# A graph network on one core: rounds of eight tables instead of twelve in the count stage

## The reference

```python
edge_index = jnp.stack([src, dst])                   # row = src, col = dst
h = jnp.maximum(_layernorm(x), 0.0)
deg = jnp.bincount(row, length=n)
norm = deg_inv_sqrt[row] * deg_inv_sqrt[col]
agg = segment_sum(norm[:, None] * h[col], row, n)    # what the count stage makes
x = x + relu(agg @ W.T + b)
h = jnp.maximum(_layernorm(x), 0.0)
edge = concatenate([h[src], h[dst], edge_attr_16])
h2 = relu(relu(edge @ W1 + b1) @ W2 + b2) @ W3 + b3
return x + h + segment_sum(h2, dst, n) / maximum(cnt, 1)[:, None]   # cnt: edges per dst
```

## Time and profile before

| | us |
|---|---|
| median of three runs | 6202.02 (6193.15 to 6207.08) |
| the profiled execution, whole | 6196.43 |
| its span, first to last instruction | 6194.6 |
| busy in the span: PE, DVE, POOL, ACT | 5140.4, 3557.7, 4065.8, 1693.7 |
| first build matmul of the count stage starts | 507.3 |
| first unit matmul starts (round 13) | 655.5 |
| units alone begin | 1949.5 |
| the stage after the count stage begins (POOL) | 2053.35 |

### The profile page before, as it was taken

One profiled execution on the slowest core, in us unless ns is written; L12 is line 12 of the kernel. 1 busy time (PEld: TensorE's weight loads), 2 busy tenths in 40 slices (PEclk: granted clock), 3 DMA queues, 4 the chain that ended last, 5 costly groups with the idle time before them and its releaser, 6 DMA issues. The chain is left out here.

```text
span 6194.6 us, 148888 instructions
## 1 busy us (share of the span) xinstructions
PE 5140.4 (83%) x40298; PEld 4289.9 (69%) x40299; DVE 3557.7 (57%) x11420; ACT 1693.7 (27%) x3084; POOL 4065.8 (66%) x3903
## 2 busy tenths in 40 slices
PE   3885999999999768887778888878888778888887
PEld 3883899999998656666666666666666666666666
DVE  8998999999996544434433443434443434443444
ACT  3226666666663221111111111111111111111110
POOL 2005666666664467777777777777777777777776
PEclk9998999999999878888888888888888888888888
DMA  9206999999999743333333333333333333333332
GB/s 164 32 0 150 272 290 288 288 291 292 289 291 266 163 112 84 84 84 85 84 84 83 85 84 84 83 85 83 85 83 85 83 85 83 85 83 84 84 85 66
DMA packets 653785, 816.41 MB, mean 132 GB/s; under 512 B 426282, under 2 KB 471052, under 8 KB 653114
## 3 DMA queue, kind: packets, MB, share of 16 engines
q1 hardware_dynamic: 478251, 592.65, 33.0%
q0 software_dynamic: 175360, 221.63, 17.2%
HBM read 563.36 MB, written 250.47 MB: 131 GB/s over the span
## 5 line engine op out<-in xcount | busy, mean ns | idle before, releaser
L1677 POOL DMA_INDIRECT p_got<-p_tab,idx_d x3128 | 2958.5, 946 | 972.2 <-issue 895.0
L1663 ACT ACTIVATE h<-z,b_col 128x512 f32<-128x512 f32 x782 | 537.4, 687 | 3390.8 <-PE z L1803 3332.8
L1667 DVE TENSOR_TENSOR h<-z,nb 128x512 f32<-128x512 f32 x782 | 540.7, 691 | 1595.2 <-PE z L1643 1582.6
L1637 PEld LDWEIGHTS z<-ident_f,p_got 128*128 128x128 f32 x3128 | 422.5, 163 | 1352.0 <-DMA p_got<-p_tab,idx_d 1185.4
L1637 PE MATMUL z<-ident_f,p_got 128*128 128x128 f32 x3128 | 601.2, 324 | 753.8 <-DMA p_got<-p_tab,idx_d 753.6
L1022 PE MATMUL a_ps<-tile_r,pair_l 128*128 128x288 fp8e5 x5280 | 1041.6, 287 | 75.8 <-DVE tile_r L1109 47.5
L859 POOL DMA_INDIRECT sum_tab<-val_s,idx_s x496 | 787.0, 1587 | 469.7 <-ACT val_s L976 331.5
L1643 PEld LDWEIGHTS z<-w_sb,h 128*128 128x128 f32 x6256 | 1044.7, 237 | 58.0
L1043 PE MATMUL out_ps<-gw,a_got 121*128 121x144 bf16 x11340 | 1078.1, 225 | 4.8 <-DMA a_got<-a_tab 4.7
L1643 PE MATMUL z<-w_sb,h 128*128 128x128 f32 x6256 | 1033.8, 320 | 0.0
L985 ACT CAST stage<-a_ps 128x576 uint16<-128x576 f32 x1320 | 837.4, 639 | 406.0 <-PE a_ps L1022 399.1
(11 more groups left out here) (200 smaller groups left out, 3693.2 us busy)
## 6 DMA issues: line engine op xcount, KB each, us to landing
a_tab<-stage SPq DMA_DIRECT2D x330, 576.0 KB
a_got<-a_tab SPq DMA_DIRECT2D x330, 576.0 KB
rel<-rel_row SPq DMA_DIRECT2D x391, 192.0 KB
p_got<-p_tab,idx_d POOLq DMA_INDIRECT x3128
ef<-in_edge_t SPq DMA_DIRECT2D x391, 64.0 KB
q_win<-q_tab SPq DMA_DIRECT2D x782, 24.0 KB
src_bc<-src_row SPq DMA_DIRECT2D x124, 128.0 KB
a_tab<-big SPq DMA_DIRECT2D x22, 472.5 KB
```

The lines of the kernel that those rows point to most:

```text
L1637: pe.matmul(out_tile, p_rows[:, j, :], ident_f[:, :], start=False, stop=False, is_transpose=True, skip_group_check=True)
L1677: pool.indirect_dma_start(p_rows[:, j, :], None, p_tab, bass.IndirectOffsetOnAxis(idx[:, j:j + 1], 0)).then_inc(landed, 16)
```

## The change

ROUND goes from 12 to 8. What follows from it:

- A round has 8 tables: two blocks of four, so two stage buffers in turn and two blocks in `a_got`, where there were three; 16 turns instead of 24; 8 gathers per super-block. `pair_l` gets four buffers instead of three.
- Tables go from 110 rounds of 12 (1320) to 154 rounds of 8 (1232), super-blocks from 10 to 14. LAG stays 13 rounds.
- The tiles left over rise: SG goes from 124 side groups to 168 (672 tiles). There is exactly one side group in each round, the double ones are gone. Groups 154 to 166 are worked on in the 13 rounds that have no tables, and group 167 behind the last round.
- The places inside a round move: pick at 4, mix at turn 10, sum at turn 14, and so on.

```diff
-ROUND = 12
+ROUND = 8
-    MORE_EACH = 7
-    two_sides = range(LAG, ROUNDS, MORE_EACH)
-    assert len(two_sides) == SG - ROUNDS and two_sides[-1] < ROUNDS
+    assert ROUNDS + LAG < SG <= ROUNDS + LAG + 1
-            pair_l = [sb(f"pair_l{k}", [P, P, 2 * WIN_TILES], BF16, life) for k in range(3)]
+            pair_l = [sb(f"pair_l{k}", [P, P, 2 * WIN_TILES], BF16, life) for k in range(ROUND // 2)]
-                PICK_AT = 6
-                MOVE_AT = 8
-                NUMBER_AT = 9
-                MIX_AT = 14
-                SUM_AT = 18
-                MIX_KEPT_AT = 6
-                VAL_KEPT_AT = 8
-                EARLY, LATE = -3, 2
+                PICK_AT = 4
+                MOVE_AT = 6
+                NUMBER_AT = 7
+                MIX_AT = 10
+                SUM_AT = 14
+                MIX_KEPT_AT = 4
+                VAL_KEPT_AT = 6
...
-                    for r in range(ROUNDS):
+                    for r in range(SG):
...
-                        for e, _ in placed(r, sides(r)):
-                            scatter(e)
+                        scatter(r)
...
-                    sweep(sp, DW, LAG - 1, sides, body)
+                    sweep(sp, DW, LAG - 1, body)
+                    for e in range(ROUNDS + LAG, SG):
+                        load_src(e)
+                        load_g(e)
...
+                            if turn_of == MIX_AT:
+                                mix_rows(r)
+                            if turn_of == SUM_AT:
+                                sum_rows(r)
...
-                    sweep(pe, DW, LAG, sides, body)
+                    sweep(pe, DW, LAG, body)
+                    for e in range(ROUNDS + LAG, SG):
+                        mix_rows(e)
+                        sum_rows(e)
...
-                        wait_past(dve, built, pair * 2 - 4)
+                        wait_past(dve, built, pair * 2 - (ROUND - 2))
...
                             if i < n:
                                 if i % 2 == 0:
                                     one_hots_l(r, i)
...
+                            if i == PICK_AT:
+                                pick_same(r)
+                            if i == MOVE_AT:
+                                move_same(r)
+                            if i == NUMBER_AT:
+                                number(r)
```

More of the change, by code:

```diff
@@ L103, in like @@
     def like(r):
[L104 to L115, removed]
-            if hi - lo == 1:
[L117 to L126, removed]
+        return (built(r), r // FOLD) if built(r) else (0, -1)
+    body(0, None, None, built(0), 0, 0)
+    for lo, hi in ((1, min(lag, FOLD)), (FOLD, lag)):
+        if hi - lo == 1:
+            body(lo, None, None, ROUND, 0, lo // FOLD)
+        elif hi > lo:
+            with eng.Fori(lo, hi) as r:
+                body(r, None, None, ROUND, 0, lo // FOLD)
+    for sb in range(units // FOLD):
+        u = sb * FOLD
+        lo = 0
+        while lo < FOLD:
+            hi = lo + 1
+            while 0 < lo and hi < FOLD and like(u + hi + lag) == like(u + lo + lag):
+                hi += 1
+            n, home = like(u + lo + lag)
+            if hi - lo == 1:
+                body(u + lo + lag, u + lo, lo, n, sb, home)
+            elif n == 0 and lo == 1 and sb == units // FOLD - 1:
                 with eng.Fori(0, (hi - lo) // 2) as t:
@@ L923, in load_g, with body @@
                                      ).then_inc(g_win_loaded, 16)
[L925 to L929, removed]
+                    def body(r, u, seg, n, sb_index, home, tail=0):
+                        following = r + 1 if isinstance(r, int) else sp.snap(r + 1)
                         for k in range(GROUPS):
-                            if len(after) == 2 and k == 0:
-                                load_src(after[0])
                             if READ * k < n:
@@ L936, in body @@
                                 load(u, seg, k, sb_index)
[L937 to L942, removed]
+                            if k == 0:
+                                load_src(following)
+                            if k == 1:
+                                load_g(following)
                     def weight(dst, src):
@@ L976, in keep_val, with body @@
                         act.copy(val_s[s][:, :, :].rearrange("p j f -> p (j f)"), sum_ps).then_inc(val_ready, 1)
-                    def body(r, side, s):
+                    def body(r, s):
                         for i in range(ROUND):
@@ L986, in body @@
                                      a_ps[:, 2 * (i % 2):2 * (i % 2) + 2, 0:PIECE]).then_inc(kept, 1)
[L987 to L996, removed]
-                        pairs = 0
-                        while r > 0 and r + 2 * pairs + 1 < ROUNDS and sides(r + 2 * pairs) == sides(r + 2 * pairs + 1) == side:
-                            pairs += 1
-                        if pairs > 1:
-                            with act.Fori(0, pairs) as t:
-                                for o in range(2):
-                                    body(act.snap(t * 2 + (r + o)), side, (s + o) % 2)
-                            r += 2 * pairs
-                        else:
-                            body(r, side, s)
-                            r += 1
+                            if i == MIX_KEPT_AT:
+                                keep_mix(r)
+                            if i == VAL_KEPT_AT:
+                                keep_val(r, s)
+                    for r in range(2):
+                        body(r, r)
+                    with act.Fori(1, ROUNDS // 2) as t:
+                        for s in range(2):
+                            body(act.snap(t * 2 + s), s)
+                    for e in range(ROUNDS, SG):
+                        keep_mix(e)
+                        keep_val(e, e % 2)
                 @block.tensor
```

40 lines of the change are left out of this document (11 added, 29 removed).

## The result

| | before | after |
|---|---|---|
| median of four runs, us | 6201.56 (6193.15 to 6207.08) | 6423.96 (6423.09 to 6428.35) |
| ratio to before | 1 | 1.0365 [1.0352, 1.0377] |
| the profiled execution, us | 6196.43 | 6424.47 |
| first build to first unit, us | 148.2 | 117.6 |
| one round with tables and a unit, us | 13.34 for 12 tables | 10.93 for 8 |

The kernel is 222 us slower, 3.65% [3.5, 3.8]. The forecast was 6480 us with a range of 6345 to 6575: the sign and the mechanism are right, the amount was 56 us too high.

What follows compares the result with a forecast made beforehand. The prediction took the wait for the second `a_got` block, a round of 11.35 us, to bound the long stretch: 113 (tables alone) + 1600 (tables and units) + 116 (units alone) against 1546 us, +283, so 6480 us, range 6345 to 6575.

Steps and rivals of the forecast that it cites:

- The cycle: Second `a_got` block, tables and units: 3.95 us PE work, 1.9 to the load's issue, 5.5 to use; a round of 11.35 us.
- The third: Last term of that round's sum: from the load's issue to the block's first use by PE, taken as 5.5 us.
- the 6.0 us of the full rounds: Issue to use of a load, read at the edge of the full rounds before the change; used for the upper bound.
- the 4.8 of the units alone: Issue to use of a load, in us, from the stretch with units alone before the change; used for the lower bound.
- the first block: First block of `a_got`: adds nothing to the round, 8.2 us of work and stall against 7.2 for issue and landing.
- my estimate of 3.35 us: Time for one 576 KB transfer by the skill's rule, 2.0 us plus bytes over 436 GB/s; the forecast said the trace contradicts it.
- Rival 1: Long stretch: load fits, under 3.5 us issue to use, DVE bounds rounds at 9.4 us; 6205 us in all, chance 0.09.
- "Nor do the saves.": Saves from the stage buffers don't lengthen the round: ACT needs a buffer again after over 7 us, landing takes at most 6.0.
- DVE's 9.4 us and PE's 8.9: Each engine's own work in a round of eight tables with a unit; both were to fit within 11.35 us.
- The fill: Stretch with tables alone, 13 rounds: 113 us, a gain of 35, with 4 us added for POOL's gathers in eight rounds.
- The end: Units alone, 13 rounds in 103 us, then the fourteenth group: 116 us in all, a loss of 12.
- Behind the stage: Combine and edge stages, after the count stage: nothing changes there.

Runs made afterwards that it cites:

- load_first: The changed kernel with SP issuing each block's load ahead of the save of the same block: 6352.57 us, ratio 1.025 to the kernel before.
- four_stage_save_first: The changed kernel with four stage buffers instead of two, save still before load: 7374.93 us on a chip where the kernel before took 7201.63.

## Why the prediction was right, point by point

**The cycle.** It was written as 3.95 + 1.9 + 5.5 = 11.35 us. The trace has 3.98 + 2.02 + 4.88. The first two terms hold to 0.1 us. The third, from the load's issue to its use, is the mis-sized one: 0.6 us too long in this cycle, 0.8 by the median of 4.7. I took it nearer to the 6.0 us of the full rounds than to the 4.8 of the units alone; in the changed kernel the DMA engines have gaps (share 0.86), and the load behaves as the one at the lower bound. That the gaps are the reason is my reading; it fits load_first, with a share of 0.94 and 6.0 us. Over 141 rounds the round of 10.93 instead of 11.35 is the 59 us by which the long stretch is shorter than forecast (1541.5 against 1600). I had put the first block at nothing; it adds its 29 us of waits. The Trainium skill, "DMA: Bandwidth & Descriptors", section on the anatomy of one DMA, states the rule behind my estimate of 3.35 us for transfers issued by GpSimd. These loads are issued by SP, so their 4.88 us neither bear it out nor speak against it, as I had written that the trace does. Rival 1, which needed a landing under 3.5 us, didn't come about.

**That this path and no other sets the round.** Shown from both sides: shortening it shortened the round (10.47), giving it a round's more room removed the wait of PE and took the round to 9.59, and taking away work of DVE, or giving the saves more buffers, the other two candidates, left the changed kernel's round within 0.15 us. The larger `a_got` ran only together with four stage buffers and the load first, never by itself in the changed kernel.

**"Nor do the saves."** Right for the changed kernel (four_stage_save_first), but with less to spare than I wrote. I gave a stage buffer over 7 us; a save that stands behind a load took 6.8 us in the case shown, so the saves became the late ones as soon as the order was turned.

**PE and DVE.** PE was to be busy about 80% and to wait some 340 us; it is 85.8% and 216.7 us in 189 waits. The waits are shorter since the round is shorter, and a PE record runs on into a stall (its end is modelled: 1521.89 plus 0.41 in the last build before 1523.92, where a pair costs 0.25), which the forecast of the share didn't consider. DVE's 9.4 us and PE's 8.9: with the path out of the way the round is 9.59 us with DVE and PE at 97%, and 9.24 with DVE's work reduced. Both are 0.2 to 0.3 us above the sums, which have no gaps in them. Rival 1's 6205 us would have been 6231 on this count.

**The fill.** 113 us forecast, 117.6 measured. The 117.6 are 109 and 8.6, and 8 is what the sum gives when POOL's longer time in the eight rounds with gathers counts in full instead of by half. DVE is busy 90% and POOL 72% of that stretch; no run separated them.

**The end.** 116 us forecast, 126.1 measured. Up to the last unit it took 101.7 us (103 forecast). Behind it I had put the scatters of the fourteenth group alone and 3 us for landing and end. The rows have the scatters of two groups there, eight of 1.85 us, and 7.02 us from the last scatter's end to the next stage. The two terms are 7.4 and 4 us too small. Mix and copies, 2.5 us in the sum, lay beside the scatters, but the last scatter of an earlier group stood in their place, 2.3 us.

**Behind the stage.** I said that nothing changes there; it is 10.2 us shorter. The combine stage, first of before, then of after, from the stage's first instruction to the first gather of the edge stage:

```profile
2053.00:2229.00 176.00, 112.25 (x590) 94.43 (x590) 102.35 (x158) 71.84 (x84) 90.74 (x60) 0.75 0.66 146
```

```profile
2291.00:2457.00 166.00, 108.99 (x590) 92.60 (x590) 100.57 (x159) 72.07 (x84) 90.98 (x60) 0.78 0.61 155
```

The same instructions and bytes in 166 instead of 176 us.

The sum then closes: 113 + 4.6, 1600 - 58.5, 116 + 10.1, less 10.2 behind, is 54 us under the 6480, against a profiled execution of 6424.5. That the three small errors cancel to 4.5 us is luck; the fourth is the mis-sized term.

## What to carry to other kernels

A pipeline whose buffers come round once per round has a path of release, issue and landing that doesn't shrink with the round: before making a round shorter, add up that path for each buffer, with the issue-to-use time from rows where an engine was seen to wait for it and the DMA share is alike (4.7 us at 0.86 here, 6.0 at 0.94), and compare it with the work between release and next use. Where it doesn't fit, the order of transfers did little here: with the load first the saves were late and the loads stayed so; more room (another set of rows, smaller blocks) takes the wait away. And then look which engine is next: here twelve tables in 13.34 us are 1.11 us a table, and eight in 9.59 are 1.20, so that even without the stall the fixed work of a round is paid more often than a shorter start wins back.

## What the runs showed of the hardware that I had not expected

- The combine stage took 164 to 168 us in each kernel with rounds of eight, on both kinds of chip (167 with the doubled `a_got`), and 174 to 176 us in each with rounds of twelve, the profile of the kernel before beside it included. Its transfers land sooner (by the median, `q_tab` 4.2 us instead of 5.1, `parts` 3.5 instead of 4.0). The size of the tables in DRAM is one thing in which these kernels differ; whether it is that was not tested.
- In load_first, a save of 576 KB behind a load of 576 KB took 6.5 us by the median from issue to the reuse of its buffer, and up to 7.8; the load in front of it took 6.0 to its use, against 4.7 in the changed kernel.
- 7.02 us pass between the end of the last indirect DMA on POOL and the first instruction of the next stage, 5.6 of them after it had landed, a wait that no row of before shows: there POOL had been done long before and the next stage followed other engines' last work.
- On one chip the kernel before took 7201.6 us with a mean granted clock of 0.83 in all of its twelve runs, on the others 6196 to 6202 at 0.905. The count stage's round was within some 0.2 us on both, with a granted clock near 1.00. In the edge stage (3000 to 5000 us) the version with the doubled `a_got` has a clock of 0.77 there and PE busy for 1510 us, where the changed kernel on the other kind has 0.87 and 1609; which of the two follows from the other isn't shown. A comparison of two kernels changed its sign between them (0.9981 and 1.0052).
